# Layer 1's last attention steps: the order of VectorE's and ScalarE's work within a step, and the place of a table load

## The reference

```python
q = (latents @ Wq).reshape(b, q_len, N_KV_HEADS, N_GROUPS, HEAD_DIM)
k = (hidden_states @ Wk).reshape(b, kv_len, N_KV_HEADS, HEAD_DIM)
v = (hidden_states @ Wv).reshape(b, kv_len, N_KV_HEADS, HEAD_DIM)
scores = jnp.einsum('bqhgd,bkhd->bhgqk', q, k) * scale
attn = jax.nn.softmax(scores.astype(jnp.float32), axis=-1).astype(q.dtype)
out = jnp.einsum('bhgqk,bkhd->bqhgd', attn, v)
return out.reshape(b, q_len, N_HEADS * HEAD_DIM) @ Wo
```

## Time and profile before

| | us |
|---|---|
| median of 3 runs | 1216.76 |
| lowest, highest | 1213.69, 1220.43 |
| the profiled execution: its own time | 1218.03 |
| the profiled execution: span from first to last instruction | 1216.7 |
| TensorE busy | 1181.7 |
| VectorE busy | 803.2 |
| ScalarE busy | 669.5 |
| GpSimd busy | 423.2 |

### The profile page before, as it was taken

How to read it: one execution, slowest core, us unless ns; L and a number is a source line. 1 busy time by engine, 2 the same in 40 slices (tenths; PEclk the granted TensorE clock), 3 DMA queues, 4 the chain that set the end, 5 groups by cost and what they waited for, 6 DMA issues and landing times.

```text
span 1216.7 us, 16554 instructions
## 1 busy us (share of the span) xinstructions
PE 1181.7 (97%) x5936; PEld 913.3 (75%) x5936; DVE 803.2 (66%) x1509; ACT 669.5 (55%) x1562; POOL 423.2 (35%) x517
## 2 busy tenths in 40 slices
PE   8899998999999999999999999999999999999999
PEld 5555555667776676788888888878888888888767
DVE  3456778677776784856666666774456666666877
ACT  2245653477777785355555555653455565556631
POOL 2503442577777783012322322320023223322300
PEclk9889999999999999999999999999999999999999
DMA  8667242685679666521111121121211121211201
GB/s 285 173 145 167 76 166 89 245 260 102 124 189 299 150 146 105 179 70 61 53 61 44 61 70 61 52 70 44 78 44 51 63 61 61 69 44 44 69 1 70
DMA packets 72849, 127.93 MB, mean 105 GB/s; under 512 B 11640, under 2 KB 30968, under 8 KB 70072
## 3 DMA queue, kind: packets, MB, share of 16 engines
q1 hardware_dynamic: 53024, 73.90, 20.0%
q0 software_dynamic: 17296, 48.26, 15.9%
q10 hardware_dynamic: 2448, 4.72, 1.1%
HBM read 150.37 MB, written 26.48 MB: 145 GB/s over the span
## 4 chain that ended last, share of the span: by engine, by line
PE 74%; POOL 7%; DVE 6%; issue 6%; DMA 4%; ACT 3%; SPq 0%; ACTq 0%; POOLq 0%; DVEq 0%
PE bank L473 48%; PE bank L2031 7%; PE bank L1223 5%; PE bank L2007 4%; POOL moe L1606 4%; PE bank L685 2%; POOL xs L1595 2%; PE bank L699 2%; PE bank L651 1%; PE bank L666 1%; POOL wf_raw L1585 1%; DMA wf_raw<-in_wffn,weight_row 1%; PE bank L2356 1%; PE bank L449 1%; PE bank L1283 1%
## 5 line engine op out<-in xcount | busy, mean ns | idle before, releaser
L1998 POOL TENSOR_SCALAR p<-p,mx 128x256 f32<-128x256 f32 x256 | 163.6, 657 | 500.4 <-DVE mx L1992 500.4
L1190 DVE TENSOR_TENSOR wf_lo<-wf_raw,wf_hi 128x512 fp32r<-128x512 f32 x188 | 121.5, 688 | 34.4 <-ACT wf_hi L1184 32.2
L1984 ACT ACTIVATE p<-bank,mx 128x256 f32<-128x256 f32 x256 | 118.1, 486 | 10.9 <-DVE mx L1974 10.8
L473 PE MATMUL bank<-xnA_hi,w1q_hi 128*128 128x512 f32 x288 | 117.7, 409 | 0.7 <-DVE w1q_lo L1773 0.7
L1184 ACT ACTIVATE wf_hi<-wf_raw 128x512 fp32r<-128x512 f32 x192 | 110.2, 626 | 10.1 <-DMA wf_raw<-in_wffn,weight_row 10.1
L473 PE MATMUL bank<-xnA_hi,w1q_lo 128*128 128x512 f32 x288 | 114.1, 396 | 0.0
L473 PE MATMUL bank<-xnA_lo,w1q_hi 128*128 128x512 f32 x288 | 113.5, 394 | 0.0
L2014 ACT ACTIVATE p1T_hi<-bank 128x512 fp32r<-128x512 f32 x128 | 75.0, 596 | 65.2 <-PE bank L2007 65.2
L1938 ACT ACTIVATE q1T_hi<-bank 128x512 fp32r<-128x512 f32 x64 | 38.3, 598 | 130.2 <-PE bank L473 130.2
L473 PE MATMUL bank<-w1o_hi,a1T_hi 128*128 128x512 f32 x256 | 105.2, 411 | 0.2 <-DVE a1T_lo L2042 0.2
L473 PE MATMUL bank<-wf_raw,zT 128*128 128x512 f32 x220 | 102.9, 593 | 2.2 <-DVE x L1266 1.7
(11 more groups left out here) (342 smaller groups left out, 2956.8 us busy)
## 6 DMA issues: line engine op xcount, KB each, us to landing
w_raw<-in_wq SPq DMA_DIRECT2D x64, 256.0 KB, 2.6
w_raw<-in_wo SPq DMA_DIRECT2D x64, 256.0 KB, 2.7
moe<-xn SPq DMA_DIRECT2D x2, 2304.0 KB, 11.7
returned<-moe SPq DMA_DIRECT2D x8, 512.0 KB, 6.4
q0st<-q_rows SPq DMA_DIRECT2D x14, 256.0 KB, 4.7
ctx<-in_ctxT SPq DMA_DIRECT2D x2, 1024.0 KB, 8.6
x<-in_x SPq DMA_DIRECT2D x8, 256.0 KB, 8.0
q_rows<-q0T_hi ACTq DMA_DIRECT2D x8, 256.0 KB
```

The lines of the kernel that those rows point to most:

```text
L473: ins = nc.tensor.matmul(ps, a, b, start=(n == 0), stop=(n == len(pairs) - 1))
L1190: nc.vector.tensor_tensor(wf[m % 2][1][:, a, c, :], raw[m % STREAMS][:, a, c, :], wf[m % 2][0][:, a, c, :].bitcast(F32), ALU.subtract).the ...
L1984: ins = nc.scalar.activation(pr1[s % 2][:, h, :], banks.of(("s1", s, n))[:, hh * 2 * P:(hh + 1) * 2 * P], ACT.Exp, bias=m[:, UH + h:UH + h ...
L1998: ins = nc.gpsimd.tensor_scalar(pr1[s % 2][:, h, :], pr1[s % 2][:, h, :], m[:, 3 * UH + h:3 * UH + h + 1], 1.0, ALU.mult, ALU.mult)
```

## The change

`LATE` is H1 - UH - 1 = 32 - 4 - 1 = 27. From pass 27 of each half on:

- VectorE writes the remainders of both parts of the turned probabilities of step i-1 ahead of the maxima of step i+1 (before: behind them).
- ScalarE splits the attended rows of step i-1 ahead of the exponentials of step i+1 (before: behind them and behind the pass's weights). VectorE's remainder of the attended rows accordingly stands ahead of the reciprocals and of the weights.
- The small square root with its table load goes from the end of half 1's pass 31 to the end of its pass 32.

```diff
+        LATE = H1 - UH - 1
...
@@ scalar_attention1, steps @@
                 if 1 <= i <= STEPS:
                     scalar_turn(s - 1, 1)
+                if LATE <= i <= STEPS:
+                    scalar_attend(s - 1)
                 if i + 1 < STEPS:
                     scalar_exp(s + 1)
...
-                if 1 <= i <= STEPS:
+                if 1 <= i < LATE:
                     scalar_attend(s - 1)
@@ vector_attention1, steps @@
-                if i + 1 < STEPS:
+                if i < LATE:
                     vector_max(s + 1)
...
                 if 1 <= i <= STEPS:
                     vector_turn(s - 1, 1)
+                if LATE <= i < STEPS - 1:
+                    vector_max(s + 1)
                 if i >= 2:
                     vector_out(s - 2)
+                if LATE <= i <= STEPS:
+                    vector_attend(s - 1)
                 if i + 1 < STEPS:
                     vector_norm_sum(s + 1)
...
-                if 1 <= i <= STEPS:
+                if 1 <= i < LATE:
                     vector_attend(s - 1)
...
         def scalar_ending(i):
-            if i == STEPS - 1:
+            if i == STEPS:
                 nc.scalar.activation(hr[:, 0:1], eps, ACT.Sqrt)
```

## The result

| | before | changed |
|---|---|---|
| median of 14 runs each, us | 1217.12 | 1223.24 |
| lowest, highest | 1213.69, 1220.43 | 1219.65, 1227.69 |
| profiled execution, own time / span | 1218.03 / 1216.7 | 1220.22 / 1218.9 |

The ratio is 1.0056, 95% interval 1.0045 to 1.0067: slower by 6.8 us (5.5 to 8.2); the two medians are 6.1 us apart. Forecast were 3.4 us more and 1220.2. The time lies in the range (1213.2 to 1224.5), but past the forecast's own (to 1222.3) and just over the 0.5% that I took for the border of no change; to no change I had given 0.78, to slower 0.17.

The account below looks back on a forecast made before the run. TensorE bounds the kernel, busy 1181.7 of 1216.7 us. Half 0's +2.4 and half 1's +1.0 give +3.4 us, 1220.2 on the median of 1216.76; range 1213.2 to 1224.5, the forecast's own 1218.3 to 1222.3.

Parts of the forecast that it names:

- The later exponentials: Half 0, pass 27: exponentials 3.46 us later delay weights and the fourth tile's load; attend 27 starts 2.0 us later.
- the term for the wait itself: Half 0, attend 27: TensorE's wait grows from 1.34 to 3.3 us.
- rival C: Late passes: remainders colliding with GpSimd's rescaling, and hops, cost each of eight passes 0.4; +6.5 us, 1223.3; chance 0.14.
- Passes 28 to 31 of half 0: Work between attends just fits, 0 twice; then +0.2 at attend 30 and +0.2 at pass 31's second turn part.
- A cover of 0.1 us: Half 0, passes 28 to 30: the path between attends needs 4.9 us, TensorE's other work takes 4.97.
- Half 1: Passes 27 and 28 +1.8 (adapters' loads later), pass 29 -0.45, pass 30 +0.85, passes 31 and 32 -1.2; together +1.0 us.
- A: Not slower: the later exponentials find a gap, attend 27 starts by 793.9; say -3 us, 1213.8; chance 0.15.
- B: A draw: half 0 pays 2, half 1's adapters' loads come no later than ScalarE needs; +0.5, 1217.3; chance 0.15.
- The table load: Half 1, passes 31 and 32: with its 1.28 us gone from before the last turn, the last wait falls, -1.2 us.

Follow-up runs that it names:

- 6: The changed kernel with half 0's fourth weight of pass 27 split in pass 28 instead (three weights in each); ratio 1.0029 to the kernel before.
- 7: The changed kernel with LATE one higher, so pass 27 of both halves stays as before; ratio 0.9988 to the kernel before.
- kernel 1: The change in half 0 alone; half 1's late passes and the table load as in the kernel before; ratio 1.0035 to that kernel.
- kernel 5: The changed kernel plus 12 overwritten matmuls into a free output bank, ahead of attend 27 of half 0; ratio 1.0044 to the kernel before.
- kernel 2: The change in half 1 alone, table load in its new place; half 0 as in the kernel before; ratio 1.0011 to that kernel.
- 10: The kernel before with only the small square root and its table load moved to the end of half 1's pass 32; ratio 0.9985 to it.
- kernel 3: The changed kernel plus 12 overwritten matmuls into attend's own bank, ahead of attend 27 of half 0; ratio 1.0083 to the kernel before.
- 9: The kernel before with only the attended rows' split and remainder moved forward; maxima and table load stay; ratio 1.0114 to the kernel before.
- 4: The kernel before with only VectorE's remainders of the turned probabilities ahead of the maxima; table load stays; ratio 1.0063 to the kernel before.

## Why the prediction was right, and where it was too small

- *The later exponentials* were the cause, by the path that I gave: the chain of the changed kernel has its links in that order, attend 27's wait became 3.57, with the 0.16 of lost overlap 3.73 (forecast 3.3), attend 27 is 2.0 to 2.3 late (forecast 2.0), and taking out the load (6) or pass 27 (7) takes out the loss at attend 27.
- *The step that failed is the term for the wait itself*: I counted a stand of 3.3 us as 3.3 us. It also brings the granted clock to the lower level for the next matmuls, 1.3 us in the changed kernel's profile and 2.6 in kernel 1's. Nothing in the profile before shows a stand of this length in the late passes. But its first 190 us have four falls, and ahead of each TensorE was at work for only part of the time: 4.86 of the 7.50 us before the one at 47.5, 6.31 of 8.00 (at 68), 3.36 of 5.50 (at 95.5) and 2.21 of 4.00 (at 184). I had not asked what the new wait would do by these rows. The direction was right, and so was the path; that the time of 1223.24 lies within the range is in part luck, since the range's upper end stood there for rival C, whose mechanism did not come, and not for the clock.
- *Passes 28 to 31 of half 0*: forecast 0, 0 and +0.4; kernel 5, without the clock's part, has +0.14, +0.28, +0.46 and +0.13. A cover of 0.1 us was none. Half 0 in sum +3.05 against +2.4, the clock left out.
- *Half 1*: forecast +1.8, -0.45, +0.85, -1.2; kernel 2 has +1.97, -0.23, +1.00, -1.24, in sum 1.5 against 1.0. The changed kernel's own profile, where the load was quick, has -0.05, -0.26, +1.01, -1.29: the three later terms near the forecast, the first not. The terms that I listed for pass 29 add up to 7.09 us and not to 7.15; the pass measured 7.34 in the changed kernel (1147.64 to 1154.98).
- *The sum* of what was measured: 3.05, then 1.3 to 2.6 for the clock, and 1.5: 5.9 to 7.2 us (more where half 1's wait of 2.7 us brings the clock down too, as in kernel 6), where the runs say 5.5 to 8.2. The forecast's 3.4 is the same sum without the clock and with 1.1 us of small terms left out. That the clock fell in most of the 14 runs, as it did in the profile of one, is not shown; the mean granted clock of the whole run had a median of 0.992 over them, against 0.994 over the five of kernel 5 and 0.994, 0.994 and 0.996 over the runs of before beside the experiments.
- *The rivals.* A needed attend 27 by 793.9; it came 2.3 late. B named the adapters' landing; the changed kernel's own profile, with the quickest of thirteen, looks like B in half 1, kernels 2 and 5 don't. C's price (6.5) was nearly right for the wrong reason: GpSimd's rescaling was 3.23 us long in pass 27 and ended at 791.98, 7 us before its turn, so it decided nothing; the pairs of remainders took 1.37 instead of 1.28 (not 0.22 more). Beside these pairs GpSimd's four rescalings took 2.79 to 3.23 us, against 1.84 in the shortest of before, most of whose rescalings in half 0 met the pairs too (2.86 to 3.21). This is the collision that the Trainium skill has in "SBUF — State Buffer", section "SBUF: two separate sides"; the trace agrees that there is one, but nearly all of its cost fell on GpSimd, which had the time.
- *The table load*: 1.28 us on the path, a term of 1.2 forecast and 1.27 measured by itself (10).

## What to carry to other kernels

Moving an instruction forward in an engine's queue makes everything behind it wait for what it waits for. Before the move, list what those others release (here a load's buffer and the loads of the next stage), and test the parts of a change by themselves as well as together: here each move alone lost, though one of them had looked like the gain. And a new wait of over 3 us on TensorE is to be priced with what it does to the clock, or filled; a fill must write a bank that is free while the wait lasts. What won here was small and took a cause away instead of reordering around it: the weight moved out of pass 27, and the table load moved off the path.

## What the runs showed of the hardware

How long TensorE stood in the late passes, and what its granted clock did then: with each stand of 3.3 to 4.7 us (the changed kernel, 1, 3 and 9) it came down to the lower level, just behind the stand (the changed kernel and 3) or already in it (1 and 9), for 3.4 us in the first two and 6.8 in the others. There a matmul of 512 columns took 0.43 us from start to start instead of 0.23. Of five stands of 2.1 to 2.9 us three were followed by a fall (2.10 in kernel 3, 2.45 in 4, 2.81 in 6) and two were not (2.72 in 2, 2.87 in 5). None of 1.8 us or less was. Kernel 5, with the longest wait filled, kept the clock there. The landing of one 256 KB load behind a 1 MB one took 5.10 to 7.26 us after its issue, over thirteen profiles. Before the first changed instruction a single profile was up to 2.9 us ahead of or behind that of before, and two of them were 5.1 us apart, most of the size of the whole effect.
